# Attention and a small feed-forward layer on 8 cores: VectorE takes 40 of 1024 exponential tiles, DMA takes over transposes, block 0 in a new order

## The reference

```python
x = x + attention(layernorm(x))     # x: 4 x 4096 x 1024, fp32
x = x + ffn(layernorm(x))

# attention: 16 heads of queries, one shared key and value of 64
q = einsum('bnd,hkd->bnhk', r, query_proj)
k = einsum('bmd,dk->bmk', r, key_proj)
v = einsum('bmd,dv->bmv', r, value_proj)
attn = softmax(einsum('bnhk,bmk->bnhm', q, k) / sqrt(64), axis=-1)
out = einsum('bnhv,dhv->bnd', einsum('bnhm,bmv->bnhv', attn, v), output_proj)

# ffn: 64 channels, each with a hidden layer of 16
s = einsum('btd,dm->btm', x, Win) + bin_
g = einsum('btmh,mh->btm', relu(s[..., None] * W1 + b1), W2) + b2
out = einsum('btm,md->btd', g, Wout) + bout
```

## Time and profile before

| | |
|---|---|
| median of 3 runs | 1017.74 us |
| the profiled execution's own time | 1017.6 us |
| its span on the slowest core | 1016.1 us |
| spans of the 8 cores | 1012.9 to 1016.1 us |
| mean granted clock of TensorE | 0.986 to 0.989 |
| busy on that core: ACT, PE, DVE, POOL | 952.2, 900.6, 358.7, 56.5 us |

### The profile page before, as it was taken

One profiled execution on the slowest core, in us unless ns is written; L12 is line 12 of the kernel. 1 busy time (PEld: TensorE's weight loads), 2 busy tenths in 40 slices (PEclk: granted clock), 3 DMA queues, 4 the chain that ended last, 5 costly groups with the idle time before them and its releaser, 6 DMA issues.

```text
span 1016.1 us, 28595 instructions; the slowest of 8 cores (1012.9 to 1016.1 us)
## 1 busy us (share of the span) xinstructions
PE 900.6 (89%) x11582; PEld 493.1 (49%) x11712; DVE 358.7 (35%) x637; ACT 952.2 (94%) x1043; POOL 56.5 (6%) x131
## 2 busy tenths in 40 slices
PE   3898899998899999998889999998889998898884
PEld 3445555555444545544444454544444554454442
DVE  4535666652512222234202122244202326424215
ACT  2597999999999999999999999999999999999981
POOL 3201111100000000000000000000000000000000
PEclk9999999999999999999999999999999999999995
DMA  8502257220000000002200000001210000400101
...
DMA packets 13406, 40.94 MB, mean 40 GB/s; under 512 B 3168, under 2 KB 3296, under 8 KB 13152
## 3 DMA queue, kind: packets, MB, share of 16 engines
...
## 4 chain that ended last, share of the span: by engine, by line
ACT 80%; issue 9%; PE 5%; DVE 3%; DMA 3%; POOL 0%; DVEq 0%; SPq 0%; POOLq 0%; ACTq 0%
ACT ptu L816 80%; DMA xtra<-x_own 2%; PE ob L457 1%; DMA xbuf<-x_own 1%; PE spa L662 1%; PE spb L662 1%; DVE r1u L478 1%; PE sda L380 0%; DVE r1t L504 0%; DVE lnst L468 0%; PE spb L695 0%; DVE lnst L469 0%; DVE gacc L787 0%; POOL rstd L838 0%; PE sdb L391 0%
## 5 line engine op out<-in xcount | busy, mean ns | idle before, releaser
L816 ACT ACTIVATE ptu<-spa 128x1024 bf16<-128x1024 f32 x512 | 594.5, 1161 | 17.7 <-PE spa L662 17.6
L816 ACT ACTIVATE ptu<-spb 128x1024 bf16<-128x1024 f32 x512 | 595.9, 1164 | 2.9 <-PE spb L662 2.9
L457 PE MATMUL ob<-vab,ptu 128*128 128x65 bf16 x8192 | 409.1, 195 | 0.7 <-ACT ptu L816 0.5
L457 PEld LDWEIGHTS ob<-vab,ptu 128*128 128x128 bf16 x8192 | 298.4, 97 | 208.4 <-issue 208.4
L662 PE MATMUL spb<-qt,k2t 64*128 64x512 bf16 x1024 | 200.8, 380 | 40.5 <-ACT ptu L816 34.9
L662 PE MATMUL spa<-qt,k2t 64*128 64x512 bf16 x1024 | 200.9, 380 | 36.5 <-ACT ptu L816 28.3
L662 PEld LDWEIGHTS spb<-qt,k2t 64*128 64x128 bf16 x1024 | 63.4, 92 | 127.2 <-issue 108.1
L662 PEld LDWEIGHTS spa<-qt,k2t 64*128 64x128 bf16 x1024 | 62.6, 92 | 114.5 <-issue 95.1
L725 DVE TENSOR_TENSOR oacc<-oacc,ob 128x520 f32<-128x520 f32 x50 | 34.8, 696 | 77.3 <-PE ob L457 77.2
L836 POOL TENSOR_SCALAR lnve<-lnmv 128x1 f32<-128x1 f32 x48 | 12.7, 264 | 658.0 <-DVE lnmv L471 658.0
L527 DVE TENSOR_TENSOR xbuf<-xbuf,sda 128x512 f32<-128x512 f32 x16 | 11.0, 688 | 93.3 <-PE sda L423 80.0
...
## 6 DMA issues: line engine op xcount, KB each, us to landing
...
wqb<-wq POOLq DMA_DIRECT2D x8, 256.0 KB, 9.6
...
out<-xbuf SPq DMA_DIRECT2D x2, 256.0 KB, 2.6
```

Source lines behind the costliest of these rows:

```text
L457: r = te.matmul(osum[:, hd, c * 65:(c + 1) * 65], ptu[:, g % NPT, hd * 512 + c * 128:hd * 512 + (c + 1) * 128], vab[:, a + i, :], start=(i ...
L816: sc.activation(ptu[:, g % NPT, :], sps[g % 2][:], AF.Exp, scale=0.125).then_inc(ex, 1)
```

## The change

1. **Fewer slots.** In blocks 1 and 2 each segment leaves chunks 8 and 24 out of the slots (`OFF`), in block 3 chunk 8: 16 + 16 + 8 = 40 tiles. 984 slots are left. For such a tile (`E`) PE writes the two heads' scores into the side banks, DVE turns them into exponentials and PE multiplies the result by the values in the segment's slot 20, 28 or 26 (`pv_off`).
2. **DVE's exponential.** K is scaled so that a score is the exponent of two times 2^23. DVE adds a bias and clamps while it empties the banks (integer output), masks out mantissa and exponent (two `tensor_scalar`), and forms a product of two quadratic factors in the mantissa and the power of two (four `scalar_tensor_tensor` of 128x1024). ACT's exponential gets a bias tile that multiplies its results by the same constant.
3. **DMA transposes.** Finished heads (31 of 32) and the normed output tiles (14 of 16) are transposed by `dma_start_transpose` from SP's queue; `ot` is left for the last head alone, `rt` goes. `r1u` has four buffers.
4. **Loads of the residual tiles** 4 to 15 move from SP's queue to POOL's, behind the four stores of the group before; `wp` is loaded in eight pieces.
5. **Block 0.** The first two slabs run over four pairs each instead of two, Q of pairs 1 to 4 stands between slab 1's transposes, K of slab 1 is formed in two parts.
6. **The planner** counts costs (hundredths of 1 us) against a slot of 92 and lets PE run late by 25, and by 75 in the first 14 slots.

```diff
-SEGS = [(0, 0, 0, 4), (0, 1, 0, 4), (0, 0, 4, 8), (0, 1, 4, 8)]
-SEGS += [(0, hp, 0, 8) for hp in range(2, NHP)]
+SEGS = [(0, hp, 4 * sl, 4 * sl + 4) for sl in range(2) for hp in range(4)]
+SEGS += [(0, hp, 0, 8) for hp in range(4, NHP)]
...
+OFF = {1: [(8, 20), (24, 28)], 2: [(8, 20), (24, 28)], 3: [(8, 26)]}
...
+SLOT = 92
+SCORES = 22
+SWITCH = 20
+HALF = 12
+PIECE = 22
+PE_LAG = 25
+TR_LAG = 6
...
+        def pv_off(te, s, o):
+            j = OFF_NO[s, o]
+            te.wait_ge(exv, j + 1)
+            for hd in range(2):
+                for c in range(4):
+                    r = te.matmul(osum[:, hd, c * 65:(c + 1) * 65],
+                                  peb[:, j % NE, hd * 512 + c * 128:hd * 512 + (c + 1) * 128],
+                                  vab[:, OFFS[s][o][0], :], start=False, stop=False, skip_group_check=True)
...
+                    v.tensor_scalar(ez_i[:, b * 512:(b + 1) * 512], bank[:], (127 - POLY_SHIFT) * 2.0 ** 23,
+                                    0.0, op0=ALU.add, op1=ALU.max).then_inc(sev, 1)
...
+                    v.tensor_scalar(em_i, ez_i, 0x7FFFFF, 0x3F800000, op0=ALU.bitwise_and,
+                                    op1=ALU.bitwise_or).then_inc(pol, 1)
+                    v.tensor_scalar(ez_i, ez_i, -0x800000, None, op0=ALU.bitwise_and).then_inc(pol, 1)
+                    v.scalar_tensor_tensor(eu, em, POLY[0], em, op0=ALU.add, op1=ALU.mult).then_inc(pol, 1)
+                    v.scalar_tensor_tensor(ew, em, POLY[2], em, op0=ALU.add, op1=ALU.mult).then_inc(pol, 1)
+                    v.scalar_tensor_tensor(ew, ew, POLY[3], ez, op0=ALU.add, op1=ALU.mult).then_inc(pol, 1)
+                    v.scalar_tensor_tensor(peb[:, j % NE, :], eu, POLY[1], ew, op0=ALU.add,
+                                           op1=ALU.mult).then_inc(exv, 1)
...
-                sc.activation(ptu[:, g % NPT, :], sps[g % 2][:], AF.Exp, scale=0.125).then_inc(ex, 1)
+                sc.activation(ptu[:, g % NPT, :], sps[g % 2][:], AF.Exp, bias=lnp[:],
+                              scale=0.125 / SCORE_SCALE).then_inc(ex, 1)
...
+                if n >= 2:
+                    v.wait_ge(otl[n % 2], heads_moved(n - 2))
...
+                for t in ts:
+                    if t + 4 < OTILES:
+                        e.wait_ge(ost[t % 4], 16 * (t // 4 + 1))
+                        e.dma_start(xbuf[:, t % 4, :], xo_r[t + 4]).then_inc(xol[t % 4], 16)
...
+            e.wait_ge(nrm, li + 1)
+            e.dma_start_transpose(dst, r1u[:, li % 4, :]).then_inc(trl[li % 4], 16)
...
+                e.dma_start_transpose(ot[:, k % 2, i, :].rearrange("p (c t) -> p c t", c=4),
+                                      on[:, n % 2].rearrange("p c t -> p (c t)")).then_inc(otl[n % 2], 16)
```

More of the change, by code:

```diff
@@ L1 @@
 import contextlib
+import math
 import numpy as np
@@ L182, in pace @@
         s = SEG_OF[g]
-        halves = len(pv_at(s, g - SEG_AT[s]))
-        for _ in range({0: 2, 2: 1, 3: 0}[halves]):
-            if head["pe"] is not None and ok(head["pe"], 1):
-                run("pe", pe, "pe1")
-        if g + 1 != SEG_AT[s + 1] and head["dve"] is not None and ok(head["dve"], 1):
-            run("dve", dve, "dve1")
-    return counts
+        halves = pv_at(s, g - SEG_AT[s])
+        want = [("sev", USE_NO["V", CHUNKS[s][h // 2] // 4, 0] + 1) for h in halves]
+        off = [o for o, (_, r) in enumerate(OFFS[s]) if r == g - SEG_AT[s]]
+        j = OFF_NO[s, off[0]] + 1 if off else 0
+        forced += force(want + [("exv", j)], "_v")
+        if off:
+            note("epv", j)
+        pe_lag = min(pe_lag + PIECE * forced, PE_LAG)
+        t = SCORES + HALF * (len(halves) + 2 * len(off)) + (SWITCH if halves or forced else 0)
+        switch = 0 if halves or forced else SWITCH
+        while head["pe"] is not None and ok(head["pe"], 1):
+            if pe_lag + t + switch + PIECE - SLOT > (PE_LAG if g >= 14 else 75):
+                break
+            run("pe", pe, "pe")
+            t += switch + PIECE
+            switch = 0
+        pe_lag = max(0, pe_lag + t - SLOT)
+        room = SLOT + (20 if g + 1 in SEG_AT else 115)
+        while head["dve"] is not None and ok(head["dve"][0], 1) and dve_lag + head["dve"][1] <= room:
+            dve_lag += head["dve"][1]
+            run("dve", dve, "dve")
+        dve_lag = max(0, dve_lag - SLOT)
+    return counts, moves
 def build_nc():
@@ L403, in pe_side @@
                                       start=(j == 0), stop=(j == DCH - 1))
+                elif kind == "E":
+                    seg, o = OFF_TILES[a]
+                    need = max(USE_NO[q] for q in queries_of(seg))
+                    yield [free, ("sev", need + 1), ("epv", a - NE + 1)]
+                    wait_ev(te, n - 2)
+                    wait_ev(te, need)
+                    c = OFFS[seg][o][0]
+                    r = te.matmul(bank[:], k2t[64 * b:64 * b + 64, c * 128:(c + 1) * 128],
+                                  queries(SEGS[seg][0], SEGS[seg][1], b), start=True, stop=True)
                 elif kind == "ot":
```

356 lines of the change are left out of this document (227 added, 129 removed).

## The result

The changed kernel took 1084.75 us (median of 4 runs, 1083.17 to 1086.84) where the kernel before took 1017.8 us beside it. The ratio is 1.0661, interval 1.0637 to 1.0685: 67 us slower, against 977 us forecast and a range that ended at 1000. The prediction was wrong in its sign.

The account below looks back on a forecast made before the run. ACT's exponentials, 0.916 us a slot, were taken as the bound. 1017.6 - 36.6 (slots) - 7.5 (block 0) - 1.6 (waits behind pieces) + 3 (heads' ends) + 2 (filled slots) = 976.9, say 977 us; range 967 to 1000.

Parts of the forecast that it names:

- 40 slots fewer: ACT's exponentials: 40 fewer at 0.916 us each save 36.6 us, all on the path, if PE and DVE keep the beat.
- Full slots and heads' ends: PE slots filled with pieces cost 2 us; `o_out` queued behind DVE's long instructions at the 24 heads' ends costs 3.
- Rival 2: DVE late: masks cost 1.22 us or heads' ends find a queue, PE waits; 988 to 994 us, chance 0.16.
- Block 0: First slots: the 6.3 us wait at slot 64 goes and the start gains 1.2 us, together -7.5.
- the 1.2 us at the start: ACT's idle time in its first 17 exponentials: 10.8 us instead of 12.0, a gain of 1.2.
- DVE's prices: DVE's eight instructions for one `E` tile take 8.03 us, 321 us for 40, on average hidden beside ACT.
- Transposes by DMA: Head and tile transposes on SP's queue: at 2.6 to 5.5 us nothing waits, so 0 was taken.
- Rivals 1 and 3: DMA transposes slow: 1, 9.6 us a tile, 988 us, chance 0.10; 3, 9.6 us a head, 1046 us, chance 0.05.
- save it work that is off the path: Transposes leaving PE: the work itself was off the path, so they save only waiting; 1.6 us counted as gone.
- Rival 4: PE at half clock after idling: 0.86 us more a slot, 48 such slots eat the gain; chance 0.02.
- the 1.6 of waits that were to go: ACT's idle time where a transposition or piece of K on PE waited for DVE: 1.6 us of 2.3 gone.

Follow-up runs that it names:

- with one piece: At most one piece beside the value products in a PE slot from slot 64, against the changed kernel without bias tile and `E` tiles: 1023.98 us.
- With 40 tiles and one piece: At most one piece in a PE slot from slot 64, against the changed kernel without bias tile and with DVE's norm behind the next bank's emptying: 1046.02 us.
- with the norm late: DVE norms a tile after emptying the next bank instead of before, against the changed kernel without the bias tile: 1008.05 us.

## Why the prediction was wrong, point by point

**40 slots fewer: the step that failed first.** "So the time is the number of slots times 0.916" was carried over to a kernel whose slot had changed. I listed in the change that ACT's exponential gets a bias tile, and gave it no price at all, neither a row nor bounds, though it is the one edit that touches all 984 instructions on the path. It cost 0.087 us each: 984 x 0.087 = 85.6 us, twice the whole gain. Shown by doing it alone (89 us) and by taking it out twice (68 and 81 us). None of the rows shown before could price it, and the sum should have said so: 41 / 984 = 0.04 us a slot was all that the gain could bear. But it is not the whole miss: without the bias tile the time was 1016.8, and the forecast would still have been 40 us short and out of its range.

**Full slots and heads' ends: the second step that failed.** I took 2 + 3 us. Blocks 1 to 3 lost 28.0 us over their beat where the kernel before lost 2.8. Without `E` tiles 10.6 of the 28.0 were there already, so some 17 go to the 40 tiles. Without the bias tile it is 39.4 for 2.8, 36.6 us, which is all that 40 slots fewer can bring; 12.6 of the 39.4 are there without a tile. In the changed kernel PE's waits for the banks of the tiles' scores come to 12.6 us:

```profile
PE sdb L507 <- DVE oacc L644: 6.5, 5, 2.2
PE sda L507 <- DVE oacc L644: 6.1, 5, 1.8
...
PE sda L515 <- DVE on L896: 1.3, 1, 1.3
```

Rival 2 had DVE late at heads' ends; there PE waited once, 1.3 us. The place was wrong: PE waits before an `E` half, for a bank that DVE is late to empty. I had counted loads (91% of DVE, 92% of PE) and not the order in which two in-order engines hand two banks to each other. The filled slots were priced by a mean of 0.93 us, where single slots of 1.11 made ACT wait.

**Block 0.** Forecast -7.5. First start +1.4, slots 0 to 16 -0.7, 16 to 64 -6.4 and 64 to 256 +0.1 us, each less 0.087 a slot for the bias tile: -5.6. That takes the bias tile's price off also where ACT waited for PE and it cost nothing. The kernel without bias tile and `E` tiles shows the order more directly: slots 0 to 16 +0.5, 16 to 64 -5.3, 64 to 256 +2.1, together -2.7 (the first start, +2.4, is within its spread). Right was the place: the wait of 6.3 us at slot 64 went. Of the 1.2 us at the start 0.2 came: ACT was idle 11.8 us in its first 17 exponentials, for 12.0 before and 10.8 forecast (10.3 with the bias tile). And the slots up to 256, taken at 0, lost 2.1 to slots with two pieces; with one piece it is 0.8.

**DVE's prices.** 8.03 us a tile was forecast. Groups of the changed kernel, to be held against the earlier trace rows:

```profile
L692 DVE SCALAR_TENSOR_TENSOR oacc<-oacc 128x1024 f32<-128x1024 f32 x40 | 48.7, 1217 | 0.0
...
L689 DVE TENSOR_SCALAR oacc<-oacc 128x1024 int32<-128x1024 int32 x40 | 27.4, 686 | 0.0
L644 DVE TENSOR_SCALAR oacc<-sda 128x512 int32<-128x512 f32 x40 | 27.4, 685 | 1.9 <-PE sda L507 0.9
```

1.22 for 1.286, 0.69 for 0.752, 0.685 for 0.69: 2 x 0.685 + 2 x 0.69 + 4 x 1.22 = 7.6 us. Right.

**Transposes by DMA.** 0 was taken, up to 9.6 us a tile feared. Their rows among the DMA issues of the changed kernel (name, queue, count, us from issue to landing), for the earlier trace rows:

```profile
ot<-on SPq DMA_TRANSPOSE x38, 2.3
...
r1t<-r1u SPq DMA_TRANSPOSE x14, 3.1
```

No wait of PE names one, and the landings are under the 5.5 us that I had as cover. Rivals 1 and 3 did not happen. The Trainium skill's 1309 ns for one 128x128 block, from VectorE: DVE Perf Modes, section The three transpose paths, does not add up over blocks here: a head of four landed in 2.3 us and a tile of eight in 3.1. What was wrong is the sentence that PE's transposes "save it work that is off the path": behind the ends of heads PE now idles in two slots running, and the lower clock follows (above). The change was not run with its transposes alone, so what this costs is read from the traces, not shown.

**The clock.** Rival 4 had 48 slots at half speed as its price, 0.86 us each, and a chance of 0.02, since "the new order idles PE less". In the changed kernel 44 distances of blocks 1 to 3 lie at the lower level, where the kernel before had none; they cost 14.5 us, 0.33 each, half of the 28.0 (waits that lie there included). So it came in number and not in price, and it is not the cause of the sign. Its premise was wrong: behind the ends of heads PE idles more than before. With 40 tiles and one piece PE waited 36.7 us at the products, and 3.7 + 3.1 for banks, 43.5 in all, and blocks 1 to 3 lost 60 us more than in the kernel with one piece and no `E` tile; 50.7 us were lost in stretches of the lower clock, but how much of it is the clock and how much the waits that lie there is not separated. That the granted clock is no part of the bias tile's price is seen in the run with the bias tile alone, where two halves of the chip had different clocks and nearly the same time (and the kernel's other three executions, with 0.979 to 0.989 on every core, took 1106.1 to 1107.2 us):

```profile
die 0 (median of its cores): 1106.2 us, clock 0.839
die 1 (median of its cores): 1102.2 us, clock 0.986
```

**The sum anew**, against the profiled run's 1085.42: 977 + 85.6 (bias tile) + 21.8 (blocks 1 to 3: 25.2 more than before, where 3.4 were taken, 3 + 2 less the 1.6 of waits that were to go) + 1.9 (block 0) = 1086.3. The two last terms are what the table leaves over, so that the sum closes is no proof of them.

**The best version.** Without the bias tile, with the norm late, one piece a slot and 24 tiles (32 do as well): 1002.1 us, 1.6% under the kernel before and 7.6% under the changed one.
